# Route mask in a gated recurrence-and-attention layer: signs turned by VectorE in place of a TensorE product

## The reference, cut to what matters

```python
x = silu(x_prev * conv_w[:, 0] + x * conv_w[:, 1])
q = silu(x @ Wq); k = x @ Wk; v = x @ Wv; g = x @ Wg      # 1024 -> 512, 512, 1024, 1024
q, k = rotary(q), rotary(k)                                # 16 heads of 32
scores = softmax(einsum(v, router_w)); onehot = one_hot(argmax(scores), 2)
norm = 1 / cumsum(onehot, axis=tokens)
qk = (q * score * norm) . (k * onehot) * HDK**-0.5         # nonzero only where query and key chose the same route
o = (qk * tril) @ v
out = (silu(g) * headnorm(o)) @ Wout
```

## Time and profile before

| | |
|---|---|
| median of 3 runs | 1711.4 us |
| the profiled execution's own time | 1711.15 us |
| its span | 1709.4 us |
| PE (TensorE) busy | 1555.0 us, 91% |
| DVE (VectorE) busy | 1482.8 us, 87% |
| ACT (ScalarE) busy | 721.3 us, 42% |
| POOL (GpSimd) busy | 602.4 us, 35% |

### The profile page before, as it was taken

One profiled execution on the slowest core, in us unless ns is written; L12 is line 12 of the kernel. 1 busy time (PEld: TensorE's weight loads), 2 busy tenths in 40 slices (PEclk: granted clock), 3 DMA queues, 4 the chain that ended last, 5 costly groups with the idle time before them and its releaser, 6 DMA issues.

```text
span 1709.4 us, 37059 instructions
## 1 busy us (share of the span) xinstructions
PE 1555.0 (91%) x15575; PEld 793.1 (46%) x15607; DVE 1482.8 (87%) x1982; ACT 721.3 (42%) x901; POOL 602.4 (35%) x716
## 2 busy tenths in 40 slices
PE   0424899999999999999999999999999999999996
PEld 0212455555555545555554555555545555555553
DVE  7888888888998888888998888889988888889932
ACT  4725434444334444444344344444344344443420
POOL 1421344333343444233343443333433443333321
PEclk9957899999999999999999999999999999999998
DMA  9500011110111111100101111100111111011000
GB/s 264 207 13 0 26 39 38 38 32 27 32 27 37 39 38 39 39 26 26 38 26 38 38 39 38 36 26 28 32 33 38 38 39 38 28 28 34 14 14 25
DMA packets 23413, 70.73 MB, mean 41 GB/s; under 512 B 2256, under 2 KB 2512, under 8 KB 23248
## 3 DMA queue, kind: packets, MB, share of 16 engines
q1 hardware_dynamic: 23248, 68.37, 13.8%
HBM read 51.59 MB, written 16.78 MB: 40 GB/s over the span
## 4 chain that ended last, share of the span: by engine, by line
DVE 70%; issue 12%; ACT 11%; PE 5%; POOL 1%; DVEq 0%; DMA 0%; SPq 0%; ACTq 0%; POOLq 0%
DVE seg L858 11%; DVE small L839 5%; DVE seg L849 4%; DVE big L313 4%; DVE fb L851 3%; ACT ek L616 3%; DVE x_ring L1013 2%; DVE big L1053 2%; DVE fa L851 2%; DVE fb L868 2%; DVE fa L1007 2%; DVE seg L1039 2%; ACT L616 2%; DVE fb L1003 2%; DVE fa L868 2%
## 5 line engine op out<-in xcount | busy, mean ns | idle before, releaser
L387 PE MATMUL ps_g<-big,h_hi 128*128 128x512 f16 x1536 | 586.6, 382 | 32.5 <-DVE small L952 26.7
L391 PE MATMUL ps_g<-big,h_lo 128*128 128x512 f16 x1536 | 586.1, 382 | 0.0
L388 PE MATMUL ps_g<-big,h_hi 128*128 128x512 f16 x1536 | 586.0, 382 | 0.0
L387 PEld LDWEIGHTS ps_g<-big,h_hi 128*128 128x128 f16 x1536 | 156.3, 102 | 173.8 <-issue 10.6
L391 PEld LDWEIGHTS ps_g<-big,h_lo 128*128 128x128 f16 x1536 | 150.9, 98 | 183.9 <-issue 4.4
L1187 POOL TENSOR_TENSOR small<-small 128x1 f32<-128x1 f32 x64 | 14.1, 221 | 611.5 <-DVE small L843 602.3
L388 PEld LDWEIGHTS ps_g<-big,h_hi 128*128 128x128 f16 x1536 | 151.0, 98 | 165.6 <-issue 4.7
L387 PE MATMUL ps_g<-big 128*128 128x512 f16 x512 | 194.5, 380 | 4.6 <-DVE big L919 1.8
L388 PE MATMUL ps_g<-big 128*128 128x512 f16 x512 | 194.2, 379 | 0.0
L391 PE MATMUL ps_g<-big 128*128 128x512 f16 x512 | 194.1, 379 | 0.0
L858 DVE TENSOR_TENSOR_SCAN seg<-decay,seg 128x1088 f32<-128x1088 f32 x64 | 179.2, 2801 | 2.2
(11 more groups left out here) (166 smaller groups left out, 2684.1 us busy)
## 6 DMA issues: line engine op xcount, KB each, us to landing
x_ring<-in_x SPq DMA_DIRECT2D x32, 512.0 KB
vx<-in_ctx SPq DMA_DIRECT2D x32, 512.0 KB
out<-x_ring SPq DMA_DIRECT2D x32, 512.0 KB
big<-in_wv SPq DMA_DIRECT2D x2, 2048.0 KB, 21.5
big<-in_wg SPq DMA_DIRECT2D x2, 2048.0 KB, 20.9
big<-in_wout SPq DMA_DIRECT2D x2, 2048.0 KB, 20.2
big<-in_wq SPq DMA_DIRECT2D x1, 2048.0 KB, 14.5
big<-in_wk SPq DMA_DIRECT2D x1, 2048.0 KB, 19.7
```

Source lines behind the costliest of these rows:

```text
L387: nc.tensor.matmul(dst[:, :], hi, hi_of(u)[:, kc * HALF:(kc + 1) * HALF], start=(kc == 0), stop=False)
L388: nc.tensor.matmul(dst[:, :], hi, lo_of(u)[:, kc * HALF:(kc + 1) * HALF], start=False, stop=False)
L391: last = nc.tensor.matmul(dst[:, :], lo, hi_of(u)[:, kc * HALF:(kc + 1) * HALF], start=False, stop=(kc == KC - 1))
```

## The change

The diff does more than the route mask. The parts are:

1. **Mask.** `same_route` and `reach` are gone. GpSimd writes the sign times `seen` (the key pattern that any query of the block reaches, from the turned causal pattern), and VectorE turns this bf16 tile of 128 x 512 by a third `turn_heads` into `sgn_t`, which `same` compares. `sgn_t` lies in `tmp`.
2. **Banks and waits.** The sign sums move from `ps_s[1]` to `ps_t[0]`; `gate_max_turn` and `sign_sums` lose waits, and `xn_transposes` gets one for `s_cum`.
3. **Squares.** `squares` moves into `tmp`, and ScalarE no longer waits for `s_up` ahead of them. VectorE waits for its own `s_ss` ahead of the rotation.
4. **Drain.** In step 31 TensorE does the values of tile 31 between the halves of the output product O0 and after it, ahead of O1. In step 32 VectorE sums the squares ahead of the two final sums of tile 30, multiplies o by the gate before the factor is there, and then applies the factor in two products of its own; GpSimd's L1244 is left out there. The last tile is stored in two halves.
5. **Preamble.** A cast and a reduction of small tiles become one reduction.

```diff
@@ sp
+                if prev2 and not prev:
+                    for g in range(2):
+                        part = slice(g * HALF, (g + 1) * HALF)
+                        after(sp, s_fin, 2 * (i - 2) + g + 1)
+                        sp.dma_start(out[:, bass.ds((i - 2) * TT, TT), part], x_ring[:, (slot + 2) % 4, part])\
+                          .then_inc(s_store, 16)
@@ pe
-                    same_route(i)
...
-                                    (lambda: values_ready(i, g)) if main and part else None)
+                                    (lambda: values_ready(i, g)) if nxt and part else None)
...
+                            if main and not nxt and g == 0:
+                                values_ready(i, part)
+                                values(i, part)
-                        if main:
+                        if main and nxt:
                             values(i, g)
...
-                nc.tensor.matmul(ps_s[1][:, 0:H], causal_m[:, :], sgn, start=True, stop=True).then_inc(s_cump, 1)
+                nc.tensor.matmul(ps_t[0][:, 0:H], causal_m[:, :], sgn, start=True, stop=True).then_inc(s_cump, 1)
-            def same_route(i):
-                after(pe, s_route, i + 1)
-                after(pe, s_cum, i + 1)
-                nc.tensor.matmul(ps_s[1][:, :], reach, route, start=True, stop=True).then_inc(s_rt, 1)
@@ act
-                    after(act, s_up, 2 * p)
@@ dve
-                if prev2:
+                if prev2 and (main or not prev):
                     final(i - 2, 1, (slot + 2) % 4)
...
+                if prev and not main:
+                    for g in range(2):
+                        final(i - 2, g, (slot + 2) % 4)
+                    for g in range(2):
+                        part = slice(g * HALF, (g + 1) * HALF)
+                        after(dve, s_gtp, 2 * p)
+                        V.tensor_tensor(o_sb[:, part], ps_o[g][:, :], sg[:, part], ALU.mult).then_inc(s_og, 1)
...
+                if prev and not main:
+                    dve.wait_ge(s_f, p + 1)
+                    for g in range(2):
+                        dve.wait_ge(s_og, g + 1)
+                        rows = by_head(o_sb[:, g * HALF:(g + 1) * HALF], DV)
+                        V.tensor_tensor(rows, rows, per_head(fac, 8 * g, 8 * g + 8, DV), ALU.mult).then_inc(s_gt, 1)
...
                     turn_heads(s_rk, i, rot_k, k_sb, s_kt)
+                    turn_heads(s_route, i, route, sgn_t, s_rt)
                     same(i)
...
-                V.tensor_tensor(by_head(same_m, BLK), by_head(ps_s[1][:, :], BLK), per_head(sgn, 0, H, BLK),
+                V.tensor_tensor(by_head(same_m, BLK), by_head(sgn_t, BLK), per_head(sgn, 0, H, BLK),
                                 ALU.is_equal).then_inc(s_same, 1)
@@ pool
+                if prev and main:
                     pool.wait_ge(s_f, p + 1)
...
-                                    fold.rearrange("p (o l) -> p o l", o=1).to_broadcast([P, H, BLK]), ALU.mult)\
+                                    seen.rearrange("p (o l) -> p o l", o=1).to_broadcast([P, H, BLK]), ALU.mult)\
```

More of the change, by code:

```diff
@@ L122, in flamingo_layer @@
         route = work[:, 3 * C:3 * C + HALF // 2].bitcast(BF16)
-        reach = work[:, 3 * C + HALF // 2:3 * C + HALF // 2 + P // 2].bitcast(BF16)
-        fold = work[:, 3 * C + HALF // 2 + P // 2:3 * C + HALF // 2 + P // 2 + BLK]
+        seen = work[:, 3 * C + HALF // 2 + P // 2:3 * C + HALF // 2 + P // 2 + BLK]
         turn = work[:, 3 * C + HALF:4 * C]
@@ L136, in flamingo_layer @@
         gt_hi, gt_lo = g_split[:, 0:C], g_split[:, C:2 * C]
-        squares = work[:, 6 * C:7 * C]
         tmp = work[:, 7 * C:8 * C]
+        squares = tmp
+        sgn_t = tmp[:, 0:HALF // 2].bitcast(BF16)
         sink = work[:, 4 * C:6 * C].bitcast(BF16)
@@ L234, in flamingo_layer @@
         s_p, s_route, s_rt, s_same = (sem(n) for n in
-            ("probs_done", "route_signs", "route_matmul", "same_route"))
+            ("probs_done", "route_signs", "route_signs_turned", "same_route"))
         s_gmt = sem("gate_max_by_batch")
@@ L244, in flamingo_layer @@
         s_fin = sem("final_done")
+        s_og = sem("output_times_gate")
         s_rg, s_y0 = sem("gate_recip"), sem("first_step_state")
@@ L358, in step @@
             def step(i, slot, main, nxt, nxt2, prev, prev2):
-                if prev2:
+                if prev2 and not prev:
[4 more added lines that the diff above has]
+                          .then_inc(s_store, 16)
+                if prev2 and prev:
                     after(sp, s_fin, 2 * (i - 1))
@@ L370, in _ @@
             pipeline(sp, step)
-            sp.wait_ge(s_store, 16 * N)
+            sp.wait_ge(s_store, 16 * (N + 1))
         @block.tensor
@@ L492, in gate_max_turn @@
                 after(pe, s_gm2, p + 1)
-                after(pe, s_same, p + 1)
+                after(pe, s_us, p)
                 nc.tensor.matmul(ps_s[1][:, H:H + 1], to_batch, gmx, start=True, stop=True).then_inc(s_gmt, 1)
@@ L497, in sign_sums @@
                 after(pe, s_sgn, i + 1)
-                after(pe, s_us, i)
-                after(pe, s_same, i)
-                nc.tensor.matmul(ps_s[1][:, 0:H], causal_m[:, :], sgn, start=True, stop=True).then_inc(s_cump, 1)
-            def same_route(i):
-                after(pe, s_route, i + 1)
-                after(pe, s_cum, i + 1)
-                nc.tensor.matmul(ps_s[1][:, :], reach, route, start=True, stop=True).then_inc(s_rt, 1)
+                nc.tensor.matmul(ps_t[0][:, 0:H], causal_m[:, :], sgn, start=True, stop=True).then_inc(s_cump, 1)
             def xn_transposes(n, main):
@@ L514, in xn_transposes @@
                         after(pe, s_th, 2 * n - 1)
+                        after(pe, s_cum, n)
                     transposes(ps_t[g], vx[:, g * HALF:(g + 1) * HALF], s_xnp, by_batch)
@@ L569, in _ @@
             nc.tensor.transpose(ps_t[0][:, 0:P], causal_m[:, :], ident[:, :]).then_inc(s_tp, 1)
-            pe.wait_ge(s_tc, 8)
+            pe.wait_ge(s_tc, 7)
             xn_transposes(0, False)
@@ L884, in step @@
                     after(dve, s_op, 2 * i)
+                    after(dve, s_ss, i)
                     rotate(dve, V, i, 0, q_sb, rot_q, s_r1q, s_rq)
@@ L895, in step @@
                     route_coefficients(i)
-                if prev:
+                if prev and not main:
[5 more added lines that the diff above has]
+                if prev and main:
                     dve.wait_ge(s_sgf, p + 1)
@@ L930, in step @@
                     conv_sum(n)
-                if prev:
+                if prev and (nxt or not main):
                     final(p, 0, (slot + 3) % 4)
@@ L951, in route_coefficients @@
                 after(dve, s_cf, i)
-                V.tensor_tensor(ctmp, ps_s[1][:, 0:H], sgn, ALU.mult).then_inc(s_cum, 1)
+                V.tensor_tensor(ctmp, ps_t[0][:, 0:H], sgn, ALU.mult).then_inc(s_cum, 1)
                 dve.wait_ge(s_cum, i + 1)
@@ L1097, in tokens_by_time @@
                 dve.wait_ge(s_tp, 5)
-                V.tensor_copy(reach, ps_t[0][:, 0:P]).then_inc(s_tc, 1)
+                V.tensor_reduce(seen, ps_t[0][:, 0:P].rearrange("p (n l) -> p l n", l=BLK), AX_X, ALU.add).then_inc(s_tc, 1)
                 V.tensor_copy(to_batch.rearrange("p (b t) -> p b t", t=TT), ident[:, :].rearrange("p (t b) -> p b t", b=NB))\
-                 .then_inc(s_tc, 1)
-                V.tensor_reduce(fold, ident[:, :].rearrange("p (n l) -> p l n", l=BLK), AX_X, ALU.add)\
                  .then_inc(s_tc, 1)
@@ L1269, in _ @@
             router_products(1)
-            pool.wait_ge(s_tc, 8)
+            pool.wait_ge(s_tc, 7)
             pipeline(pool, step)
```

## The result

The changed kernel took 1720.8 us (median of 8 runs, 1718.85 to 1721.95), the kernel before on the same chip 1713.8 us (8 runs, 1710.64 to 1714.97). The ratio is 1.0044, 95% interval 1.0034 to 1.0055: 7.5 us slower (the two medians lie 7.0 us apart). The forecast was 9.5 us slower, 1720.6 us, counted from 1711.15 us. The profiled execution took 1719.3 us with a span of 1717.5 us, 8.1 us more than the span before.

The account below looks back on a forecast made before the run. The prediction took a VectorE and ScalarE loop of 48.31 us as the bound. Third transpose +19.2, step 31 -0.4 and drain -9.3 gave +9.5 us on 1711.15: 1720.6 us, range 1710 to 1729 us.

Parts of the forecast that it names:

- What bounds the kernel: Steady step: a closed loop of VectorE and ScalarE holds 48.31 us; TensorE, though busier, does not set the pace.
- The third transpose: VectorE, between the turn of k and `same`: 0.62 us, paid in full 31 times, +19.2 us (bounds +11.2 and +25.1).
- The wait moved: TensorE's wait goes from same_route ahead of G0 to O0 and grows to about 1.2 us a step, costing nothing.
- Step 31: The step without recurrence, where TensorE is the bound: the product and its wait go, -0.4 us.
- Costed at nothing: `same` from SBUF, squares without their wait, moved banks, changed waits, GpSimd's product and the preamble: no effect.
- The drain: From the last values of tile 31 to the end: earlier transposes, better clock and halved store give -9.3 us.
- the half store: End of the drain: only half of the last store remains behind the last final sum, -2 us (bounds 0 and -3.2).
- The failed step: TensorE's clock in the drain: with 3 us idle it should keep most of it, -0.9 us (bounds 0 and -1.5).
- TensorE is the bound: Rival: the second loop, through same_route and TensorE, sets the pace; faster, 1684.3 us, chance 0.08.
- The bf16 transpose is cheap: Rival: VectorE's new transpose takes 0.36 us, 11.2 us in all; no change, 1712.6 us, chance 0.11.
- The drain gives little: Rival: VectorE's added products or the clock eat half the drain's gain; about 1725.5 us, chance 0.08.
- The collision with GpSimd: Rival: the new transpose falls beside GpSimd's work, each costing 1.63 us more, some 50 us; 1771 us, chance 0.02.

Follow-up runs that it names:

- e3: The changed kernel without the third turn, `same` comparing the unturned pattern (so another mask), and without same_route: 1704.3 us, ratio 0.9955.
- e5: The changed kernel with 4 more 512-column matmuls on TensorE ahead of G1 in each step, their result overwritten: 1720.7 us, ratio 1.0050.
- e4b: The changed kernel with the third turn done twice, the first time into a part of `tmp` that nobody reads: 1747.6 us, ratio 1.0214.
- e6: The changed kernel with 8 more 512-column matmuls on TensorE ahead of G1 in each step, their result overwritten: 1734.9 us, ratio 1.0133.
- e2: The changed kernel with the mask part undone: same_route is back, the moved squares, drain and halved last store stay: 1704.5 us, ratio 0.9952.
- e11: The changed kernel with 12 more 512-column matmuls in step 32, ahead of the transposes, result unread: 1719.2 us in one execution.
- e12: The kernel of e2 with 12 more 512-column matmuls in step 32, whose result nobody reads: 1702.0 us, ratio 0.9948.
- e8: The changed kernel with two heads' signs packed as 32-bit words, so the third turn moves 256 words: 1712.3 us, ratio 0.9995.
- e7: The changed kernel with VectorE's sum of squares moved behind all of the recurrence's denominator terms: 1818.2 us, ratio 1.0614.
- e9: The changed kernel with the transpose of ek ahead of the sum of squares and the copy of the carry behind: 1727.1 us, ratio 1.0086.

## Why the prediction held, and where its terms were off

**What bounds the kernel: right.** The loop of VectorE and ScalarE sets the pace. The three idle stretches kept their sizes; cutting `same_route` without adding a turn (e3) left the period at 48.31; 0.86 us of added TensorE work (e5) cost nothing.

**The third transpose: right in kind, 0.10 us a step too dear.** The step took 0.62 us for it, and it measured 0.52: 30 periods gave 15.5 us in place of 18.6. Two things make the difference. The instruction takes 670 ns in place of 702, and the last turn now stands 0.03 us ahead of `same`, where the turn of k stood with 0.11 us of gap. The prediction said that this wait "only moves"; it nearly vanished, and e3, without the new turn, has it back. The full price, 0.60 us, shows in e4b, where the second turn adds nothing but itself. Why the gap closes behind the third turn is not settled. The rule of the Trainium skill that was weighed there (page "VectorE: DVE Perf Modes", section "Rules for kernel authors") gives dense bf16 several times the rate for copies and products; it does not carry over to this transpose: 670 ns against 702. The 0.71 us estimated from the same page's "The three transpose paths" was the nearer of the two.

**The wait moved as forecast.** The wait ahead of G0 is gone and 1.17 us stand ahead of O0, for 1.2 forecast. e5 and e6 confirm it as true slack.

**Step 31: -0.1 in place of -0.4.** From its sum of squares to V only 0.1 us went.

**Costed at nothing: one small miss.** Step 0 lies ahead of the first sum of squares and has a transpose too, yet that sum starts 0.1 us earlier than before. Neither that transpose nor the shorter preamble shows: the sum starts at 182.5 us without the transpose (e3) and with neither of the two (e2), and the first sums of the other runs scatter from 182.2 to 183.4. So step 0's 0.62 us was counted as paid where it seems to cost nothing; where it is absorbed is not shown.

**The drain: -7.2 in place of -9.3.** The reordering gave 9.45 - 2.77 = 6.7 us, for 6.4 forecast. The end behind the last final sum went from 1709.4 - 1703.06 = 6.34 us to 1717.5 - 1713.10 = 4.4 us, so the half store gave 1.9, for 2 forecast. **The failed step is the clock:** "With 3 us of idle time it should keep most of its clock: -0.9 us (bounds 0 and -1.5)". It kept nothing of it, and the term lies outside its bounds, on the other side: about +1.4 us. From the start of the transposes to the end of the last final sum it was 1703.06 - 1688.62 = 14.4 us before and 1713.10 - 1697.28 = 15.8 now. The transposes took 1.97 us again, and nine slow matmuls stand behind them. Before, the granted clock of TensorE was back at 0.92 in the window behind the transposes:

```profile
1691.20:1697.10 5.90, 5.86 (x26) 2.61 (x27) 0.69 (x1) 0.02 (x1) 0.00 (x0) 0.92 0.00 0
```

where the changed kernel still has 0.50 for the first 3.9 us. e11 and e12 show that the term would have been met had the idle time been filled: that stretch is 13.5 us in both, 0.9 less than before.

The errors have opposite signs: up to V +15.3 us (15.5 - 0.1 - 0.1) for a forecast of +18.8, in the drain -7.2 for -9.3. So the sum came out nearer, 9.5 us for the 8.1 of the two profiled executions, than its terms did. That 1720.6 lies 0.2 us from the median of 1720.8 is luck on top: the sum started from 1711.15 us, and the kernel before had a median of 1713.8 us beside the changed one, 2.6 us more.

**The rivals.** "TensorE is the bound" fell with e3. "The bf16 transpose is cheap" fell with the 670 ns; e8 shows what it would have looked like, at 1712.3 us where 1712.6 was worked out for it. "The drain gives little" did not come out: it gave 7.2 us, above the half. The collision with GpSimd didn't happen at this place, but e7 and e9 show that it happens at others, at up to 2.1 us an instruction.

## What to carry to other kernels

Read a trade between engines by which of them is on the loop, not by which is busiest: here the engine at 91% had 1.2 us of slack a step and the one at 87% had none, and the idle stretches of the less busy one said so. Where such a change moves work off an engine, look where that engine's wait reappears, and at how long it is: 1.2 us of idle time left TensorE its clock here, and 1.7 us or more did not always. Before work is moved into idle time, look for the next thing that the engine will wait for: in e9 it left 0.8 us of a lead of 1.0. And take a change of many parts apart: this one was a loss and a gain, and the gain alone beat both kernels.

## What the runs showed of the hardware that was not expected

- **TensorE's clock after idle time.** Waits of 1.17 to 1.55 us once a step left the granted clock at 1.00 (the changed kernel, the whole loop). Behind those of 1.72 to 1.78 us it fell to the 1.2 GHz level in seven of 26 steps (e4b), behind those of 2.77 and 2.78 us in 15 of 21 (e7), and the drains' 2.66 us and 9.13 us were followed by 0.50. With matmuls that nobody reads in the gap it stayed at 1.00 (e11, e12).
- **VectorE and GpSimd on small operations.** A 64-column copy took 2.37 us in place of 0.30, and a 16-column product of GpSimd 2.26 us in place of 0.22, each as long as the other engine's large instruction lasted (e7). The Trainium skill, page "SBUF — State Buffer", section "SBUF: two separate sides", states an exclusive lock on a shared pair of ports, held for a whole instruction; the trace agrees, since each small instruction ends with the large one that began ahead of it (within 0.1 us).
- **A block transpose is priced by elements, hardly by bytes.** 128 x 512 takes 702 ns in f32 and 670 in bf16; the same bf16 data as 128 x 256 words takes 403 (e8).
- **The first period, and what is left open.** The first period varied from 48.6 us (before) to 52.0 (e7), and the clock is a part of it: in e2, e3, e4b, e7 and e11 (50.2 to 52.0 us) TensorE waited 2.0 to 3.1 us there and its granted clock fell, in e2 to 0.51 from 206.0 to 209.5 us. It did not fall in the kernel before (48.6), in the changed kernel (48.9), nor in e5 (50.0) and e8 (49.7), where TensorE waited 2.2 and 2.8 us. Why the wait itself varies is not explained, and neither are single periods that are 0.3 to 0.35 us longer than the rest in most of the kernels. The first period limits what one execution can tell to some 2 us.
